# Attention with a mixture of experts: VectorE instead of GpSimd adds the probabilities of the last key group of each half of the queries

## What is computed

```python
S = jnp.einsum('hid,hjd->hij', K, Q) * SCALE
delta = idx[:, None] - idx[None, :]
decay = jnp.where(delta < 0, 0.0, -delta.astype(jnp.float32) ** ALPHA)
S = jnp.where(delta < 0, -jnp.inf, S) + decay
C = jax.nn.softmax(S, axis=-1)
attn = jnp.einsum('hij,hjd->hid', C, V)
```

## Time and profile before

| what | us |
|---|---|
| median of 3 timed runs | 3671.74 |
| lowest and highest of them | 3670.55, 3674.10 |
| profiled execution, its own time | 3667.42 |
| its span (first to last instruction) | 3665.6 |
| granted TensorE clock, mean | 0.934 |
| steps 4 to 31 of `attend` | about 630 to 3208 |

### The profile page before, as it was taken

The page is one execution under the profiler, slowest core; times in us unless marked ns, Lnnn a source line. Parts: engine busy times, 40 slices in busy tenths (PEclk is TensorE's granted clock), DMA queues, the critical chain, the costliest instruction groups (busy, mean ns, idle before and its releaser), DMA issues. The chain is left out here.

```text
span 3665.6 us, 61864 instructions
## 1 busy us (share of the span) xinstructions
PE 3231.0 (88%) x20358; PEld 1668.7 (46%) x20366; DVE 2201.1 (60%) x5978; ACT 1204.0 (33%) x2733; POOL 1757.7 (48%) x988
## 2 busy tenths in 40 slices
PE   4567999999998999989998999989999998687998
PEld 2334444444444444444444444444444444255775
DVE  6843444566646664666466746674667567755564
ACT  3661333233333332333333323332333233311111
POOL 5640454455545554555455535553555355643222
PEclk8878999999999999999999999999999998888999
DMA  5762200011111001100100010101010100205996
GB/s 186 298 257 74 84 30 18 30 75 55 54 65 50 18 22 47 35 13 16 53 22 29 13 56 16 36 13 53 18 35 13 53 18 12 71 5 161 257 257 149
DMA packets 121804, 253.60 MB, mean 69 GB/s; under 512 B 38748, under 2 KB 39388, under 8 KB 118928
## 3 DMA queue, kind: packets, MB, share of 16 engines
q1 hardware_dynamic: 77152, 200.36, 16.2%
q0 software_dynamic: 44048, 49.26, 5.2%
q10 hardware_dynamic: 288, 0.00, 0.0%
HBM read 144.61 MB, written 202.16 MB: 95 GB/s over the span
## 5 line engine op out<-in xcount | busy, mean ns | idle before, releaser
L966 POOL TENSOR_TENSOR a_first_probs<-a_first_probs,a_probs 128x2048 f32<-128x2048 f32 (+3 forms) x320 | 1030.4, 3220 | 1044.4 <-ACT a_probs L1046 956.1
L1192 DVE CUSTOM_DVE_ANT_0 a_unused<-a_ps_ring,a_work 128x512 bf16<-128x512 f32 (+3 forms) x1536 | 778.3, 554 | 843.1 <-PE a_ps_ring L1541 838.8
L1046 ACT ACTIVATE a_probs<-a_ps_ring 128x512 f32<-128x512 f32 (+3 forms) x1280 | 508.8, 473 | 472.4 <-PE a_ps_ring L1575 297.8
L1565 PE MATMUL a_ps_ring<-a_k_t,a_q_t 32*128 32x512 f32 (+3 forms) x3072 | 440.2, 543 | 112.8 <-DVE a_row_max L1192 89.7
L1541 PE MATMUL a_ps_ring<-a_q_t,a_k_t 32*128 32x512 f32 (+3 forms) x3072 | 390.9, 550 | 14.4 <-DVE a_row_max L1192 12.5
L977 POOL DMA_INDIRECT d_slots<-a_rows,a_place_i x349 | 355.1, 1018 | 70.8 <-issue 62.4
L1565 PEld LDWEIGHTS a_ps_ring<-a_k_t,a_q_t 32*128 32x128 f32 x3072 | 158.9, 188 | 314.0 <-DVE a_row_max L1192 137.5
L1541 PEld LDWEIGHTS a_ps_ring<-a_q_t,a_k_t 32*128 32x128 f32 x3072 | 144.0, 191 | 285.7 <-issue 259.8
L1588 PE MATMUL a_ps_heads<-a_probs,a_values 128*32 128x512 f32 (+3 forms) x2560 | 269.1, 494 | 0.0
L973 POOL TENSOR_TENSOR a_attn_t<-a_attn_t,a_sum_inv 128x512 f32<-128x512 f32 x64 | 84.9, 1327 | 380.4 <-DVE a_sum_inv L1207 380.3
L1046 ACT ACTIVATE a_first_probs<-a_ps_ring 128x512 f32<-128x512 f32 x256 | 135.7, 604 | 373.6 <-PE a_ps_ring L1575 348.6
(11 more groups left out here) (289 smaller groups left out, 4430.5 us busy)
## 6 DMA issues: line engine op xcount, KB each, us to landing
d_hidden<-e_hidden SPq DMA_DIRECT2D x8, 2048.0 KB, 8.8
d_normed_t<-e_normed_t SPq DMA_DIRECT2D x8, 2048.0 KB, 11.8
a_work<-d_normed_t SPq DMA_DIRECT2D x7, 2048.0 KB, 7.9
a_hidden<-d_hidden SPq DMA_DIRECT2D x56, 256.0 KB, 2.7
out<-a_hidden SPq DMA_DIRECT2D x56, 256.0 KB
d_slots<-a_rows SPq DMA_DIRECT2D x32, 408.8 KB, 5.5
x_rows<-d_slots SPq DMA_DIRECT2D x32, 408.8 KB
x_w_gate<-w_gate SPq DMA_DIRECT2D x16, 512.0 KB, 6.4
```

The lines of the kernel that those rows point to most:

```text
L966: nc.gpsimd.tensor_tensor(total_of, total_of, probs_of(m)[:, :, 0:width], ALU.add).then_inc(added, 1)
L1046: nc.scalar.activation(probs_of(m)[:, h, 0:width], score_bank(m, h)[:, 0:width], ACT.Exp).then_inc(exp_done, 1)
L1192: nc.vector.tensor_tensor_reduce(unused[:, (HG * k + h) % N_UNUSED, 0:width], row_bank(k, h)[:, 0:width], decay[:, at:at + width], 1.0, NE ...
L1565: nc.tensor.matmul(score_bank(m, h)[:, 0:width], q_t[st.g][dims, j * P:(j + 1) * P], k_t[st.g][dims, i0:i0 + width], start=True, stop=False)
```

## The change

The groups 3 and 11 (`NARROW`) are added on VectorE by a new `add_narrow`, behind the row maxima (and ahead of the inversions, the second tail events and dense C) of the same group. GpSimd keeps the other eight adds (`WIDE`) with `added`; the new adds count `narrow_added`. `soften` and `sum_probs` wait for the semaphore that belongs to the group in question. Since the adds of a half go into the same tile, VectorE waits for GpSimd's add of the group before. Group 3 is followed by no add in its half, nor is 11. The scatters, the exponentials and all else stay where they are.

```diff
-ADDS = N_GROUPS - 2
-EARLY_ADDS = HALF_GROUPS - 1
+NARROW = (3, 11)
+WIDE = tuple(m for m in range(N_GROUPS) if m not in NARROW and GROUPS[m][1] > 0)
@@ GpSimd, add_probs
-                if j == 0:
+                if m not in WIDE:
                     return
                 if j == 1:
                     pool.wait_ge(attended, N_GROUPS * st.s + m)
                 at = slice(HALF - width, HALF)
                 pool.wait_ge(exp_done, ITEMS * st.s + HG * (m + 1))
-                wait_from_1(pool, added, ADDS * st.s + later(m))
+                wait_from_1(pool, added, len(WIDE) * st.s + WIDE.index(m))
@@ ScalarE, soften
-                        act.wait_ge(added, ADDS * st.s + k + 1)
+                        of = group_of_later(k) if k >= 0 else group_of_later(k + N_GROUPS - 2)
+                        s = st.s if k >= 0 else st.s - 1
+                        if of in WIDE:
+                            act.wait_ge(added, len(WIDE) * s + WIDE.index(of) + 1)
+                        else:
+                            act.wait_ge(narrow_added, len(NARROW) * s + NARROW.index(of) + 1)
@@ VectorE
+            def add_narrow(st, m):
+
+                half, j, i0, width = shape(m)
+                n = NARROW.index(m)
+                dve.wait_ge(exp_done, ITEMS * st.s + HG * (m + 1))
+                if m - 1 in NARROW:
+                    wait_apart(dve, narrow_added, len(NARROW) * st.s + n, passed)
+                else:
+                    wait_apart(dve, added, len(WIDE) * st.s + WIDE.index(m - 1) + 1, passed)
+                total_of = first_probs[half][:, :, HALF - width:HALF]
+                nc.vector.tensor_tensor(total_of, total_of, probs_of(m)[:, :, 0:width], ALU.add).then_inc(narrow_added, 1)
@@ VectorE, step
                     if st.rows:
                         row_maxima(st.s + 1, m)
+                    if m in NARROW:
+                        add_narrow(st, m)
                     for piece in range(PIECES):
@@ TensorE, sum_probs
-                pe.wait_ge(added, ADDS * s + (ADDS if half else EARLY_ADDS))
+                pe.wait_ge(narrow_added, len(NARROW) * s + sum(1 for m in NARROW if half or m < HALF_GROUPS))
```

More of the change, by code:

```diff
@@ L769, in attend @@
         rows_full, rows_done, max_done = sem("rows_full"), sem("rows_done"), sem("max_done")
-        scores_full, exp_done, attended, added = (sem(n) for n in ("scores_full", "exp_done", "attended", "added"))
+        scores_full, exp_done, attended, added, narrow_added = (
+            sem(n) for n in ("scores_full", "exp_done", "attended", "added", "narrow_added"))
         heads_taken, sums_inverted, heads_done = sem("heads_taken"), sem("sums_inverted"), sem("heads_done")
```

## The result

The changed kernel takes **3650.98 us** (median of 5 runs, 3647.69 to 3657.75) beside 3671.74 for the kernel before (5 runs, 3669.16 to 3676.57). The ratio is 0.9943, 95% interval 0.9929 to 0.9958: 20.8 us faster, where -6.6 was forecast; the range ended 1 us above the result.

What follows compares the result with a forecast made beforehand. TensorE, busy 88% of the span, was taken as the bound, waiting for VectorE at group 11. Release -8.6, push +4.8 and last step -2.8 made -6.6 us: 3665.1 us, range 3652 to 3677.

Steps and rivals of the forecast that it cites:

- these losses: Group 11: L1372, held by GpSimd's add, loses 0.53 us in most steps, 0.31 in head group 0; removing the add ends this.
- undamped 12.0: Group 11: the gain from L1372's release if the half clock took nothing back, 2.2 + 2.9 + 13 x 0.53 us.
- beside a scatter L1376 keeps its usual 0.50: Group 11: the scatter left behind group 10's add was to leave L1376 at 0.50 us, so no gain there.
- If the clock rises at the same moment as before ... 0.27 stays: Head groups 2 and 3: of 0.53 us released, half is lost at half clock; 13 x 0.27 = 3.5 us gained.
- the damping of 3.4: Head groups 2 and 3: half clock was to cut the whole release from 12.0 to 8.6 us.
- Rival 1: First "down": less idling brings the full clock back sooner, 1.8 us in half the 20 steps, about 3647 us; chance 0.13.
- The push of 0.61 stalls TensorE by 0.37.: Behind group 11, the new add delays L1380 and the dense bank in head groups 0 and 2: 13 x 0.37 = 4.8 us lost.
- Group 3: VectorE's new add behind group 3: room of 0.6 us in head group 0, idling of 4.13 elsewhere; cost nothing.
- The last step: Step 31, GpSimd the bound: 1.4 us gained at group 3 and another 1.4 at group 11, sum 2.8.
- the forecast of -3.8: Steps 4 to 31 without the last step's share: release of 8.6 us against a push of 4.8.
- Rival 2: Dense bank and `normalise`: the push outweighs the release from an add of 1.0 us; 3677.9 us at 1.33; chance 0.11.
- Rival 3: L1372 slow for its own reason, or half clock takes all back: +2.0 us is left, 3673.7; chance 0.14.

Runs made afterwards that it cites:

- e1: Changed kernel with only group 11's add on VectorE, group 3's back on GpSimd: 3649.70 us, 0.9951 of the kernel before.
- e2: Changed kernel with only group 3's add on VectorE, group 11's back on GpSimd: 3669.79 us, 1.0002 of the kernel before.
- e5: Kernel before, no add moved; GpSimd holds its add of group 11 until VectorE finished L1376, in steps with a tail: 3642.78 us, 0.9929 of the kernel before.
- e6: Kernel before plus 16 unneeded matmuls of 128 columns on TensorE, once, in step 3: 3638.06 us, 0.9999 of the kernel before.
- e11: Kernel before with GpSimd's add of group 11 held until L1376 is through, in head group 1's steps only: 3629.15 us, 0.9977 of the kernel before.
- e8: As e5, and GpSimd also begins its multiply and add of group 10 only behind VectorE's CAST L1301: 3580.10 us, 0.9841 of the kernel before.
- e7: As e5, plus 10 unneeded matmuls on TensorE ahead of the first "down": 3641.50 us, 0.9911 of the kernel before.
- e0: The changed kernel measured again without an edit: 3649.92 us, 0.9948 of the kernel before.
- e4: Kernel before with GpSimd's scatter at group 11 issued ahead of its add, not behind it: 3638.06 us, 1.0000 of the kernel before.
- e14: As e8, plus 10 unneeded matmuls on TensorE ahead of the first "down": 3564.83 us, 0.9792 of the kernel before.

## Why the prediction was wrong

The direction and the place were right, and so was the reason: L1372 was held by GpSimd's add. The size was off by 14 us, in these steps:

1. **"Without the add on GpSimd these losses go."** Right: L1372 at 0.43 in every step up to 30; undamped 12.0. e1, e2 and e5 show that it is the hold, and group 11's alone.
2. **"What is left behind the add of group 10 is one scatter, and beside a scatter L1376 keeps its usual 0.50."** The step that failed first. 0.50 was not L1376's own time but its time beside the scatter that stood behind the add; alone it takes 0.29. With the add gone the scatter starts 2.3 us ahead of L1372. 27 x 0.2 = 5.4 us missed (step 31 is in the last step's sum). The earlier trace rows gave L1374's durations; the same view of before would have told it of L1376, too:

```profile
L1376 DVE TENSOR_SCALAR a_inner_t<-a_inner_t x56: 293/496/5081, 704.4 to 3199.3; 128x256 f32<-128x256 f32 x56
```

   Its shortest is 0.293, its median 0.496. Together 17.4 released; TensorE's wait for L1308 fell by 15.5 over the span, the last step's 1.4 among them, since in five steps of head group 2 TensorE arrives earlier and waits 2.85 where it waited 2.53.
3. **"If the clock rises at the same moment as before ... 0.27 stays", and in head groups 0 and 1 all of it.** The moment was the same in step 13 (the low stretch ends at 1563.83, before at 1563.90), but two things in this step were wrong. First, it counted only the step's own release. TensorE was there already 0.96 ahead of the kernel before and with the 0.73 released 1.69; so 5.41 us from the start of the first "down" lay in the low stretch and not 3.79, and the 1.62 more give back half, 0.81. All of the 0.73 was gone again. Second, the path: step 13 is of head group 1, whose second "down" was to wait for L1380 and keep all. It stands directly behind TensorE's own row scores, before and after, and these took 1.96 instead of 1.16, since more of them ran at half clock (in step 12, of head group 0, 1.88 instead of 1.14):

```profile
1563.82 1.16 PE L1541 MATMUL a_ps_ring<-a_q_t,a_k_t 32*128 32x512 f32 x8
1564.90 1.98 PE L1640 MATMUL a_ps_dense<-a_sd,a_inner_t 128*128 128x512 f32 x4
```

```profile
1562.13 1.96 PE L1561 MATMUL a_ps_ring<-a_q_t,a_k_t 32*128 32x512 f32 x8
1564.02 1.98 PE L1660 MATMUL a_ps_dense<-a_sd,a_inner_t 128*128 128x512 f32 x4
```

   But the clock did not keep its pattern afterwards: at the turn to step 14, 1.43 came back, at its end 0.89. Over steps 4 to 29 the half clock was granted for 17.0 us less, and TensorE's busy time is the same within 2.4 us (+0.6, -1.0, +2.1, +2.4 in the four profiles). So the damping of 3.4 is not there in the sum, and no gain of the clock either. Rival 1 had the clock coming back sooner at the first "down"; in the changed kernel's first profile its first matmul ran at half clock throughout in 27 of 28 steps. Why the pattern changed is not settled: e6 speaks against a mere shift, e11 and e8 against the release directly ahead of it.
4. **"The push of 0.61 stalls TensorE by 0.37."** Mechanism and count right (13, weight load waits 0.35), size wrong: the hand-over is 0.74 here, and so 0.15 each, 2.0 us instead of 4.8. The 0.96 of the earlier trace rows was no hand-over: the L1640 at 1479.88 stood directly behind TensorE's row scores, which ended at 1479.95 (the row below). Where TensorE does idle for this instruction of VectorE, as in e7's step 15, it is 0.74 again (L1382 at 1727.60, the matmul at 1728.34).

```profile
1478.81 1.14 PE L1541 MATMUL a_ps_ring<-a_q_t,a_k_t 32*128 32x512 f32 x8
```

5. **Group 3**: nothing, right (e2).
6. **The last step**: forecast -2.8, of which 1.4 at group 3. At group 11 the first "down" of step 31 waits 3.59 instead of 4.96, 1.4 as forecast. Of group 3's share nothing can be told: from the first exponential of step 31 to that "down" it took 60.3 us before and 58.1, 59.9, 61.5 and 58.0 in the four profiles of the changed kernel, and e1, without group 3, ends no later than e0 in the medians.
7. **Not in the sum at all**: ScalarE's stall, 3.6 us at the 3670 level.

The sum again, against the forecast of -6.6: -5.4 (L1376), -2.8 (push) and -3.6 (stall) make -18.4, and without the damping of 3.4 it is -21.8. The four measurements lie between -18.5 and -24.0. For steps 4 to 29 the same terms turn the forecast of -3.8 into -15.6, or -19.0 without the damping, where the profiles have -14.9 to -18.3. These sums were made up afterwards; that the hold at group 11 is the cause is shown by the experiments, the split among the terms is argued from the traces.

Rival 2 (the push outweighs) needed an add above 1.0 us; it took 0.687 in the median, 0.755 at the longest. Of the fp32 add the Trainium skill (VectorE: DVE Perf Modes, the section on the TRN2 errata) gives 691 ns for 512 columns, and the trace agrees. Rival 3 falls with L1372. The Trainium skill (SBUF — State Buffer, Who interferes with whom) lists `copy`, `cast`, `tensor_scalar` and, against a GpSimd instruction that reads SBUF, VectorE instructions with two SBUF inputs as those that can contend with GpSimd for a shared pair of ports; the second to start "fully blocks". For the add against the product and the CAST the rows agree (0.96, 3.65); beside a scatter L1376 was not blocked for the scatter's 1.00 but lost 0.2. And e4's product of 2.02 started 0.43 ahead of the add, beside a scatter, and was held all the same; no run separates what the scatter and the add did there.

## What to carry over

When a change takes an instruction off an engine, list every instruction of the neighbour engine in the stretch with its shortest and its median duration, not only the one that is plainly too long: what stands behind the removed instruction moves too. Take "usual" durations from the shortest record of the same line. When a hand-over is read from a pair of records, look whether the second engine was busy with something else until then. And ask whether the work must be moved at all: a wait of one semaphore on the engine with room (e5, e8) gave more than the move.

## What the runs showed of the hardware that I had not expected

- A CAST of 128x64, 0.20 us by itself, takes 3.65 beside a multiply and an add of GpSimd that follow each other; it waits through both.
- A scatter of GpSimd makes a SBUF to SBUF TENSOR_SCALAR of 128x256 0.50 instead of 0.29 long.
- In sessions in which the kernel before takes 3669 to 3674 us, ScalarE stands still for 1.1 us in group 2 of a step, and no longer if the scatters ahead of it go out later: 16.8 us. In those in which it takes 3638 to 3639 no kernel shows the stall. 17 us of the difference lie in steps 4 to 29 (2428.1 and, in e6, 2410.9), 13 between step 31's first "down" and `experts` (145.3 and 131.9).
- TensorE's half clock: 105 us instead of 281 in steps 4 to 31 when two holds of VectorE are gone and ten small matmuls run while TensorE waits (e14).
- 17 us less at half clock do not make TensorE's busy time shorter by themselves: 2250.0 and 2250.6 us in steps 4 to 29.
